# Second feed-forward product: the last 42 rows of both output halves on the two 64-row halves of TensorE's array

## The reference, cut to what matters

```python
h = (h - mu) / jnp.sqrt(var + 1e-05) * lg + lb
h = h @ w1 + b1
a, g = jnp.split(h, 2, axis=-1)
h = a * jax.nn.gelu(g, approximate=False)      # (tokens, 682)
x = x + h @ w2 + b2                            # w2: (682, 256)
```

## Time and profile before

| | |
|---|---|
| runs | 3716.48, 3716.68, 3718.03 us |
| the profiled execution's own time | 3718.55 us |
| its span, first to last instruction | 3716.3 us |
| PE busy | 3587.9 us, 97% |
| PE weight loads busy | 2439.0 us, 66% |
| DVE, ACT, POOL busy | 2668.0, 2230.2, 766.6 us |
| mean granted clock of TensorE | 0.983 |

### The profile page before, as it was taken

One profiled execution on the slowest core, in us unless ns is written; L12 is line 12 of the kernel. 1 busy time (PEld: TensorE's weight loads), 2 busy tenths in 40 slices (PEclk: granted clock), 3 DMA queues, 4 the chain that ended last, 5 costly groups with the idle time before them and its releaser, 6 DMA issues.

```text
span 3716.3 us, 58542 instructions
## 1 busy us (share of the span) xinstructions
PE 3587.9 (97%) x20454; PEld 2439.0 (66%) x20454; DVE 2668.0 (72%) x7188; ACT 2230.2 (60%) x5084; POOL 766.6 (21%) x882
## 2 busy tenths in 40 slices
PE   4899999999999999999999999999999999999987
PEld 2566666666666666666666666666666666666665
DVE  2577777777777777777777777777777777777654
ACT  1356656656656656656666656666666666665653
POOL 1122222122221222221212221212222212222111
PEclk7799999999999999999999999999999999999999
DMA  5111111101111101111101111101111101111000
GB/s 146 24 24 24 29 30 29 23 14 24 29 30 30 26 11 24 30 30 30 29 13 18 30 30 30 29 13 18 30 30 29 29 18 13 30 29 24 7 6 9
DMA packets 104608, 99.34 MB, mean 27 GB/s; under 512 B 15276, under 2 KB 103040, under 8 KB 104320
## 3 DMA queue, kind: packets, MB, share of 16 engines
q1 hardware_dynamic: 104320, 95.61, 14.5%
HBM read 35.80 MB, written 8.39 MB: 12 GB/s over the span
## 4 chain that ended last, share of the span: by engine, by line
PE 91%; DVE 3%; ACT 2%; issue 1%; SPq 1%; POOL 1%; DMA 0%; ACTq 0%; DVEq 0%; POOLq 0%
PE ps L1040 15%; PE ps L940 12%; PE ps L1053 9%; PE ps L1016 6%; PE ps L954 6%; PE ps L1007 5%; PE ps L987 5%; PE ps L996 4%; PE ps L845 3%; PE ps L855 3%; PE ps L974 3%; PE ps L798 3%; PE ps L827 3%; PE ps L808 3%; PE ps L880 2%; PE ps L790 2%
## 5 line engine op out<-in xcount | busy, mean ns | idle before, releaser
L605 POOL TENSOR_TENSOR inv<-ssq_f,minus_half 128x16 f32<-128x16 f32 x128 | 419.9, 3280 | 907.5 <-DVE ssq_f L1255 907.5
L1040 PE MATMUL ps<-feed_area,w_s 128*128 128x256 f32 x2560 | 591.9, 382 | 5.9 <-DVE feed_area L1319 4.8
L703 ACT ACTIVATE attn_area<-attn_area,f_nb,inv 128x128 f32<-128x128 f32 (+1 forms) x1024 | 546.5, 537 | 10.4 <-DVE f_nb L1283 9.2
L1040 PEld LDWEIGHTS ps<-feed_area,w_s 128*128 128x128 f32 x2560 | 480.5, 191 | 105.8 <-issue 29.3
L1192 DVE TENSOR_REDUCE c_mx<-ps 128x2 f32<-128x512 f32 x512 | 349.2, 689 | 167.2 <-PE ps L827 163.6
L656 ACT ACTIVATE cond_area<-ps 128x512 f32<-128x512 f32 x512 | 293.7, 594 | 200.0 <-PE ps L845 199.2
L725 ACT ACTIVATE feed_area<-ps,b_s 128x256 f32<-128x256 f32 x320 | 151.1, 472 | 391.7 <-PE ps L1040 360.5
L1053 PE MATMUL ps<-feed_area,w_s 128*128 128x256 f32 x1536 | 355.8, 381 | 10.8 <-DVE feed_area L1329 10.8
L1279 DVE CUSTOM_DVE_ANT_0 attn_area<-ps,cst 128x128 f32<-128x128 f32 (+1 forms) x1024 | 303.8, 353 | 74.1 <-issue 72.1
L445 DVE COPY attn_area<-ps 128x384 f32<-128x384 f32 x256 | 142.1, 555 | 269.6 <-PE ps L996 269.6
L1053 PEld LDWEIGHTS ps<-feed_area,w_s 128*128 128x128 f32 x1536 | 281.6, 190 | 59.0 <-DVE feed_area L1329 23.4
(11 more groups left out here) (156 smaller groups left out, 6427.5 us busy)
## 6 DMA issues: line engine op xcount, KB each, us to landing
cond_area<-cond_area SPq DMA_DIRECT2D x384, 128.0 KB, 4.7
x_rows<-in_x SPq DMA_DIRECT2D x32, 256.0 KB, 2.8
f_rows<-in_fside_BxSxS SPq DMA_DIRECT2D x32, 256.0 KB, 3.2
res_rows<-in_x SPq DMA_DIRECT2D x32, 256.0 KB, 2.8
out<-res_rows SPq DMA_DIRECT2D x32, 256.0 KB, 2.1
wqkv_s<-in_L_ffn_wqkv SPq DMA_DIRECT2D x2, 1536.0 KB
w_s<-in_L_ffn_w SPq DMA_DIRECT2D x2, 1364.0 KB
cond_area<-cond_area SPq DMA_DIRECT2D x128, 6.0 KB
```

What stands on the lines that cost most here:

```text
L605: nc.gpsimd.tensor_tensor(inv[:, l, t, :], ssq_f[:, l, t, :], minus_half[:, :], ALU.pow).then_inc(SL[l]["inv_norm"], 1)
L703: nc.scalar.activation(soft[:, h % SOFT, lo:hi], soft[:, h % SOFT, lo:hi], ACT.Exp, bias=f_nb[:, l, q, h:h + 1], scale=inv[:, l, q, h:h + ...
L1040: last = mm(ps[:, N0 + f % 2, c * N:(c + 1) * N], w1_s[:, l, k, lo:lo + P], hn[:, k, :], start=(k == 0), stop=(k == KD - 1))
```

## The change

`down` 0 and `down` 1 multiply the five full blocks each. The sixth block of both halves is multiplied at the end of `down` 1: half 0 on rows 0 to 63 of the array, half 1 on rows 64 to 127. For that the last 42 rows of `w2` are loaded once per half, to partitions 0 and 64, and DVE writes the last block of `hid` twice, to partitions 0 and 64. `down` 1 waits for all seven `geglu` ahead of its first matmul; `down` 0 for five. `w2_out` is counted up at the end of each half, both in `down` 1.

```diff
-    rstd=1, normed=1, w1_out=HK, gelu=HK, geglu=HK,
+    rstd=1, normed=1, w1_out=HK, gelu=HK, geglu=HK + 1,
...
-        LAYER_LOADS = 12 * DEPTH + 3
+        LAYER_LOADS = 13 * DEPTH + 3
...
-                load(w2_s[0:HREST, l, HFULL], w2[l, HFULL * P:HID], layers_loaded)
+                for m, lo in enumerate((0, GREST)):
+                    load(w2_s[lo:lo + HREST, l, HFULL, m * P:(m + 1) * P], w2[l, HFULL * P:HID, m * P:(m + 1) * P], layers_loaded)
...
                 elif name == "down":
                     m = t
-                    for f in range(HK):
-                        if m == 0 and f in (0, HFULL):
-
-                            pe.wait_ge(SL[l]["geglu"], upto(seq, "geglu", HFULL if f == 0 else HK))
-                        last = mm(ps[:, N0 + m, 0:N], w2_s[:, l, f, m * P:(m + 1) * P],
-                                  hid[:, f, :], start=(f == 0), stop=(f == HK - 1))
-                    last.then_inc(SL[l]["w2_out"], 1)
+                    pe.wait_ge(SL[l]["geglu"], upto(seq, "geglu", HFULL if m == 0 else HK + 1))
+                    for f in range(HFULL):
+                        mm(ps[:, N0 + m, 0:N], w2_s[:, l, f, m * P:(m + 1) * P], hid[:, f, :],
+                           start=(f == 0), stop=False)
+                    if m == KD - 1:
+
+                        for j in range(KD):
+                            r = GREST * j
+                            mm(ps[:, N0 + j, 0:N], w2_s[r:r + GREST, l, HFULL, j * P:(j + 1) * P],
+                               hid[r:r + GREST, HFULL, :], start=False, stop=True).then_inc(SL[l]["w2_out"], 1)
...
-                    V.scalar_tensor_tensor(hid[0:rows, f, :], ps[0:rows, N0 + f % 2, at:at + N],
-                                           b1_s[0:rows, l, b_at:b_at + 1], gate[0:rows, f % 2, :],
-                                           op0=ALU.add, op1=ALU.mult).then_inc(SL[l]["geglu"], 1)
+                    for lo in (0,) if f < HFULL else (0, GREST):
+                        V.scalar_tensor_tensor(hid[lo:lo + rows, f, :], ps[0:rows, N0 + f % 2, at:at + N],
+                                               b1_s[0:rows, l, b_at:b_at + 1], gate[0:rows, f % 2, :],
+                                               op0=ALU.add, op1=ALU.mult).then_inc(SL[l]["geglu"], 1)
```

## The result

The changed kernel is slower: 3725.44 us (17 runs, 3722.12 to 3730.84) against 3717.47 for the kernel before in runs of the same series (17 runs, 3713.53 to 3721.68). The ratio is 1.002, with a 95% interval of 1.0014 to 1.0027. The forecast was 3704, with a range of 3697.5 to 3712; that it would be slower had a chance of 0.06. The profiled execution of after took 3723.08 us, with a span of 3721.0.

What follows compares the result with a forecast made beforehand. PE, busy for 97% of the span, was taken as the bound. A gain of 14.0 us less 1.0 for loads and 0.3 for later `w2_out` gave 12.7, so 3705.85, or 3704.0 as median; range 3697.5 to 3712.

Steps and rivals of the forecast that it cites:

- Parts 1 and 2: PE's down steps: the pair gains 0.23 us at each of 61 places, 14.0 us; `down` 1's later wait costs nothing.
- C: At the pair, the two halves run one behind the other, losing 0.20 us each time: 3730 us; chance 0.06.
- D: The `weigh` behind the pair pays a second switch and load, leaving 0.03 of 0.23 us: 3716.2 us; chance 0.07.
- Part 3: DVE's second write adds 0.38 us, covered ahead of PE by about 0.1 in layer 0, 0.1 to 0.3 in layer 1.
- Rival B: DVE's second write delays PE at score 9 or head 5's turning, losing layer 0's 6.7 us: 3710.7; chance 0.12.
- Part 4: Half 0's later `w2_out` makes nothing late in DVE's down steps, except last sequence and end passes: 0.3 us in all.
- Part 5: One more DMA load per layer on SP delays PE's first score by 1.0 us, bound 0 to 6.

Runs made afterwards that it cites:

- E2: The changed kernel without the second write of hid's last block, leaving 42 rows of output half 1 out of the sum: 3713.12 us, ratio 0.998.
- E9: The changed kernel without the second write, with both last blocks on rows 0 to 63, one behind the other: 3735.11 us, run once.
- E10: The changed kernel without the second write, with the 64-row pair ahead of the second down step's five full blocks: 3714.58 us, run once.
- E7: The changed kernel with DVE's second write going to partitions 0 to 41 instead of 64 to 105: 3711.48 us, run once.
- E1: The changed kernel with DVE handling both output halves in its second down step: 3720.51 us, 1.0007 of the kernel before.
- E3: The kernel before with only DVE's second write of hid's last block added: 3722.63 us, 1.0008 of the kernel before.
- E8: The changed kernel with DVE's write to partitions 64 to 105 placed ahead of the one to 0 to 41: 3727.46 us, run once.
- E4: The kernel before with half 0's last block moved, as a full block, to the end of the second down step: 3722.03 us, ratio 1.0012.

## Why the prediction was wrong

**Parts 1 and 2, right for the body.** The unit prices held: 0.43 gained in the first step, 0.20 given back in the second, 0.46 in a pass; E2 has 0.455. That the two halves work at once was read correctly from the scores step, and E9 shows that without it C's price would have been paid. That the change behind the pair is shared with the `weigh` held too, and E10 shows what it costs when it is not. Rivals C and D fall.

**Part 3, wrong in its size and its place.** The step that failed is "a second one adds 0.38". I took it from two operations that write to the partitions that they read from. The added one writes to others, and it makes DVE 0.56 us late in layer 0 and 0.62 in layer 1; in E7, on the same partitions, it is the 0.39 of the forecast, and the pass is 110.512. With it the body would have kept nearly all of its gain, 0.42 of 0.46. I had given score 9 as the place, with 0.1 us of cover; by rows 9 the chain starts at 1540.59 - 0.53 + 0.38 = 1540.44 and not at 1540.3, which leaves 0.03. PE comes to `prob` 0 first, which needs the maximum one before, and waits 0.21 there. The cover in layer 1 was 0.1 to 0.3 by my own working, so the same 0.2 us of missed cost used it up as well. Rival B had the mechanism and even the point from which it decides (0.5 us), but its price was bounded at layer 0's gain. It ate both layers', 0.48 us in each of the 29 passes, or 13.9 us and not 6.7; E2 stands 12.3 to 13.7 us below the changed kernel. With a cover of 0.1 us, on a price taken from another form of operation, B deserved more than a chance of 0.12.

**Part 4, wrong.** "So nothing is late" was read from the order of the body and applied to all passes. The first three passes have orders of their own, and in one of them DVE's first down step stands ahead of work that PE needs. That costs 4.9 to 6.3 us by E1's times, and 4.4 by the traces' stretch around it (89.0 us in after, 84.5 in E1), of which up to 1.7 is the clock. The end passes were looked at and this was not.

**Part 5, too dear.** SP issues one load more in layer 0, but the four issues for `w1` and `w2` took 5.80 us where three took 5.42, and PE's first score waited less than before, by the timeline of after:

```profile
58.33 1.04 PE L828 MATMUL ps<-cond_area 97*128 97x256 bf16 x4 [17.94 <-DMA cond_area<-cond_area]
```

It starts 0.3 us later than in before, not 1.0. While the DMA engines had a busy share of 0.95 or more (12 to 21 us in before), SP's issues took longer than their usual 0.47, and one more did not add its own length: the issue behind layer 0's weights and four bias loads, `b_s`, starts at 24.52 in after and at 24.67 in before. What holds the issues there is not shown; so "when the queue was full", in the prediction, is a guess. Layer 1's additional load did move SP, by 0.2 us.

**The sum as it was.** Forecast: 14.0 gained, 1.3 lost. Shown: 0.02 us lost in a pass, 0.6 in 27, and 4.9 to 6.3 at the start; of the 8.0 us between the medians this leaves 1.1 to 2.5 for the last passes and for the spread between executions, less than E3's unexplained 3.8. The two profiled executions are only 4.7 us apart: 2.8 ahead of the body, 1.2 in it and 0.7 behind it. Ahead of the body after loses more than this in the stretch with the block, and is 2.2 us shorter in the one before it (from 122 us on), with 20 us at the lower clock there against 26. I have not settled that part.

## What to carry to other kernels

When a change frees one engine and puts a little work on another, look at the first wait behind the added work, with the freed engine already arriving early, and take the added price from an operation of the same form, the partitions of its output included. A count that is raised later must be followed through every written order, those of the first and last passes too; what stands behind the waiting instruction in one order may stand ahead of it in another. Put a split-array step beside one that is split already.

## What the runs showed of the hardware that was not expected

A VectorE operation that reads partitions 0 to 41 and writes 64 to 105 starts 0.50 us after its neighbour and holds the next one off for 0.51 (after, E8), where the same operation with its output on partitions 0 to 41 has 0.39 on both sides (E7). Its own duration stays at 0.47 to 0.48 us, so the page's mean duration does not show it; only the distance between starts does.

The same block of DVE at the start, with PE idle for 2.4 to 2.9 us, was followed by 3.4 us at the lower clock in after, by 6.8 in E2 and by none in E4; E1, without the block, has 1.00 from 234 to 252 us. So whether the clock falls there differs between kernels, and it decides over up to 1.7 of the 4.4 us that after loses in this stretch.
